# A two-layer graph network on one core: softmax operations for two groups at once, shorter tile-number loads, and a reordered turn start

## The reference

```
h = relu(layernorm(x))
# layer 0
xn = layernorm(h) * ln_w + ln_b
w_phys = (silu(rbf @ w1 + b1) @ w2 + b2) * cutoff[:, None]          # one record per edge
Q, K, V = xn @ wq + bq, xn @ wk + bk, xn @ wv + bv                  # 8 heads of 32
scores = sum(Q[row] * K[col], -1) / sqrt(32) * cutoff[:, None]      # per edge and head
attn = softmax(scores, axis=1)                                      # over the 8 heads of one edge
combined = xn[col] * w_phys + gate * (attn[..., None] * V[col])
x = x + h + segment_sum(combined, row) @ wo + bo
# layer 1
h = relu(layernorm(x)) @ W                                          # 4 heads of 64
e = leaky_relu(h_l[row] + h_r[col])                                 # softmax over the edges of a node
x = x + segment_sum(softmax_by_row(e)[:, :, None] * h[col], row)
```

## Time and profile before

| | us |
|---|---|
| median of 3 runs | 2323.9 |
| profiled execution | 2321.69 |
| its span | 2319.9 |
| PE busy, share of the span | 1961.0 (85%) |
| DVE busy | 1784.6 (77%) |
| ACT busy | 1479.1 (64%) |
| POOL busy | 1409.6 (61%) |

### The profile page before, as it was taken

One profiled execution on the slowest core, in us unless ns is written; L12 is line 12 of the kernel. 1 busy time (PEld: TensorE's weight loads), 2 busy tenths in 40 slices (PEclk: granted clock), 3 DMA queues, 4 the chain that ended last, 5 costly groups with the idle time before them and its releaser, 6 DMA issues.

```text
span 2319.9 us, 42068 instructions
## 1 busy us (share of the span) xinstructions
PE 1961.0 (85%) x9839; PEld 1426.4 (61%) x9840; DVE 1784.6 (77%) x4372; ACT 1479.1 (64%) x5220; POOL 1409.6 (61%) x1393
## 2 busy tenths in 40 slices
PE   5999999999958899998988889837777877877874
PEld 3777777777747677777777777624444444544542
DVE  5655444444359999998999999667999989999987
ACT  1585555555567777777777777446666666666660
POOL 0377777666776666665666664247666666666660
PEclk9999999999989999999999999977999989998997
DMA  8534444333389888888889882034433333343311
GB/s 279 160 133 144 157 146 146 138 138 131 113 291 301 299 290 292 298 293 280 296 290 308 291 296 76 19 93 113 110 107 107 105 108 100 105 110 104 106 32 56
DMA packets 162185, 403.69 MB, mean 174 GB/s; under 512 B 46887, under 2 KB 59099, under 8 KB 162108
## 3 DMA queue, kind: packets, MB, share of 16 engines
q0 software_dynamic: 79360, 276.09, 36.8%
q1 hardware_dynamic: 82748, 126.67, 17.4%
HBM read 343.89 MB, written 84.72 MB: 185 GB/s over the span
## 4 chain that ended last, share of the span: by engine, by line
PE 39%; DVE 28%; issue 16%; DMA 8%; ACT 4%; DVEq 4%; POOL 2%; SPq 0%; ACTq 0%; POOLq 0%
PE ps L1405 15%; DMA arena<-sorted_edges 6%; DVE gmx L1297 5%; PE ps L1391 4%; PE ps L1518 3%; PE ps L1521 3%; DVE arena L1329 3%; PE ps L1456 3%; PE ps L1533 2%; DVE work L1292 2%; DVE sc L1139 2%; DVE arena L1125 2%; DVEq L350 2%; PE ps L1643 2%; DVE arena L1132 2%
## 5 line engine op out<-in xcount | busy, mean ns | idle before, releaser
L630 POOL DMA_INDIRECT arena<-node_row,idxC x464 | 485.6, 1047 | 233.2 <-issue 136.8
L563 POOL DMA_INDIRECT sorted_edges<-work,pos_i x416 | 405.5, 975 | 236.5 <-issue 118.9
L1405 PE MATMUL ps<-w_sb,arena 128*128 128x256 f32 x1664 | 388.7, 386 | 0.2 <-ACT arena L674 0.2
L1643 PE MATMUL ps<-arena,hq 128*128 128x260 f32 x928 | 279.3, 428 | 96.2 <-DVE work L1292 92.8
L1069 DVE TENSOR_TENSOR work<-ps,b_bc 128x512 f32<-128x512 f32 x208 | 143.6, 691 | 273.6 <-PE ps L1405 273.6
L1405 PEld LDWEIGHTS ps<-w_sb,arena 128*128 128x128 f32 x1664 | 307.5, 190 | 72.2 <-issue 32.5
L585 POOL DMA_INDIRECT work<-node_kvx,idxB x232 | 245.7, 1059 | 154.4 <-DVE arena L1156 54.2
L585 POOL DMA_INDIRECT arena<-node_kvx,idxB x232 | 244.1, 1052 | 144.2 <-issue 51.2
L684 ACT ACTIVATE work<-work 128x256 f32<-128x256 f32 x416 | 187.5, 500 | 209.5 <-DVE work L1069 209.4
L1518 PE MATMUL ps<-arena,work 128*128 128x256 f32 x928 | 256.5, 400 | 59.1 <-issue 52.1
L1297 DVE TENSOR_REDUCE gmx<-ps 128x4 f32<-128x1024 f32 x232 | 282.5, 1218 | 28.4 <-PE ps L1618 28.4
(11 more groups left out here) (216 smaller groups left out, 3786.1 us busy)
## 6 DMA issues: line engine op xcount, KB each, us to landing
arena<-sorted_edges SPq DMA_DIRECT2D x232, 260.0 KB, 4.7
work<-sorted_rows SPq DMA_DIRECT2D x58, 256.0 KB, 3.6
arena<-in_edge_attr SPq DMA_DIRECT2D x25, 512.0 KB
node_kvx<-arena SPq DMA_DIRECT2D x24, 384.0 KB, 2.5
arena<-node_row,idxC POOLq DMA_INDIRECT x464, 3.3
sorted_edges<-work,pos_i POOLq DMA_INDIRECT x416, 2.5
sorted_edges<-arena SPq DMA_DIRECT2D x25, 260.0 KB
sorted_edges<-arena SPq DMA_DIRECT2D x1, 6240.0 KB
```

Source lines behind the costliest of these rows:

```text
L563: pool.indirect_dma_start(rec_dram[:, :], bass.IndirectOffsetOnAxis(ap=pos_i[:, 4 * q + c:4 * q + c + 1], axis=0), recA[:, q % 8, c, :], N ...
L630: pool.indirect_dma_start(row1_g[:, st.slot(16), j, :], None, row1_dram[:, :], bass.IndirectOffsetOnAxis(ap=idxC[:, batch(st).slot(4), st. ...
L1405: ins = pe.matmul(ps[:, 5 + t, half * H:(half + 1) * H], hidT[:, r, m, half, t * P:(t + 1) * P], w2_sb[:, m, :], start=m == 0, stop=m == 1)
L1643: ins = pe.matmul(agg1[r], oneh1[:, r16, j, :], msg1[:, r, j, :], start=j == 0, stop=j == GJ - 1)
```

## The change

In layer 0:

- The maximum over the heads, the exponentials, the reciprocal and the attention weights are taken for two groups at a time. DVE takes the maximum (one instruction over four columns) at the end of every even step, ACT the four exponentials in the odd step, DVE the reciprocal and the weights in the odd step. `msgA` is now made for the group five back (m), `msgP` still for the one four back; so PE's sums move from five back to six back, the addition to `acc0` from six to seven, and `msgP` has four slots, two of them in memory that held constants of the first stage (`mlp_only`). DVE runs one step longer at the end.
- DVE now adds to `acc0` ahead of the reciprocal, where before the reciprocal came first.
- DVE loads four tile numbers every fourth step instead of eight every eighth. PE loads one number every step, behind L1521's matmuls (`tile_of`), instead of eight at the first step ahead of L1518.
- `AHEAD` goes from 2 to 1: ACT copies a group's node numbers one step ahead of its one-hot matrix, not two. SP's load of records waits for `qk_cut` too.

In layer 1 DVE begins a turn's first step with the maxima; the load of tile numbers and the addition follow (`add_group` is the addition as it was).

The step ahead, and SP's load:

```
-AHEAD = 2
+AHEAD = 1
...
             def load_rec(st):
                 if not st.first(8):
                     sp.wait_ge(s("msgP_ready"), st.n - 7)
+                    sp.wait_ge(s("qk_cut"), st.n - 7)
```

The loads of tile numbers, and the new names that the code below calls:

```
-        def tiles_of(eng, k, lag, count=8):
+        def tiles_of(eng, k, lag, first):
...
-                gt_i[0:1, bass.ds(k * 8 + (16 - lag), count)], engines=(eng,), min_val=0, max_val=NT - 1,
+                gt_i[0:1, bass.ds(k * 8 + (16 - lag + first), 4)], engines=(eng,), min_val=0, max_val=NT - 1,
...
+        def tile_of(eng, k, lag, u):
+
+            _, values = nc.values_load_multi_w_load_instructions(
+                gt_i[0:1, bass.ds(k * 8 + (16 - lag + u), 1)], engines=(eng,), min_val=0, max_val=NT - 1,
...
+        def pair0(st):
+            return Step(st.k, st.u // 2, 4, NG // 2)
+
+        def msgP_of(st):
+            r = st.slot(4)
+            return msgP[:, r, :, :] if r < 2 else mlp_only[:, 2 * r - 4:2 * r - 2, :]
```

ACT in layer 0:

```
-                e = st.back(4)
-                if e.real():
+                if st.u % 2 and st.back(4).real():
+                    e = pair0(st.back(4))
                     act.wait_ge(s("sc_ready"), e.n + 1)
                     if not e.first(2):
                         act.wait_ge(s("attn"), e.n - 1)
...
+                    for r in (st.back(5).slot(4), st.back(4).slot(4)):
+                        for j in range(GJ):
+                            ins = act.activation(pe_[:, r, j, :], sc[:, r, j, :], ACT.Exp, bias=smax[:, r, j:j + 1],
+                                                 accum_out=psum_[:, r, j:j + 1])
                     ins.then_inc(s("exp0"), 1)
```

DVE in layer 0, from behind `msgP` on:

```
-                if st.u == 0:
-                    tiles[6] = tiles_of(DVE, st.k, 6)
+                if st.u % 4 == 0:
+                    tiles[7] = tiles_of(DVE, st.k, 7, st.u)
                 if a.real():
                     dve.wait_ge(s("qk"), na + 1)
                     dve.reduce_sum(sc[:, ra, :, :], heads(prod), axis=AX.X).then_inc(s("qk_sum"), 1)
-                if b.real():
-                    dve.wait_ge(s("exp0"), nb + 1)
-                    dve.reciprocal(prec[:, :], psum_[:, rb, :]).then_inc(s("prec"), 1)
                 if c.real():
...
                     dve.tensor_tensor(acc, acc, ps[:, 3 + c.slot(2), 0:H], ALU.add).then_inc(s("acc0_done"), 1)
...
+                if not both_in and b.real():
+                    e = pair0(b)
+                    re = m.slot(4)
+                    dve.wait_ge(s("exp0"), e.n + 1)
+                    dve.reciprocal(prec[:, :, :], psum_[:, re:re + 2, :]).then_inc(s("prec"), 1)
+                if not both_in and b.real():
+                    dve.wait_ge(s("prec"), e.n + 1)
...
+                if m.real():
+                    if not both_in:
+                        dve.wait_ge(s("attn"), pair0(m).n + 1)
+                    if not m.first(2):
+                        dve.wait_ge(s("agg0_ready"), m.n - 1)
...
+                if both_in and a.real():
+                    r0 = b.slot(4)
                     dve.wait_ge(s("qk_cut"), na + 1)
...
+                    dve.tensor_reduce(smax[:, r0:r0 + 2, :], sc[:, r0:r0 + 2, :, :], AX.X, ALU.max,
+                                      negate=True).then_inc(s("sc_ready"), 1)
```

PE in layer 0:

```
-                if st.u == 0:
-                    q_tiles[2] = tiles_of(PE, st.k, 2)
-                c = st.back(5)
+                c = st.back(6)
...
                     ins.then_inc(s("agg0_ready"), 1)
+                next_tile = tile_of(PE, st.k, 2, st.u)
                 b = st.back(2)
```

DVE in layer 1:

```
-                if st.u == 0:
-                    tiles[8] = tiles16(DVE, st.k, 11, 0)
                 c = st.back(11)
-                if c.real():
...
+                if c.real() and st.u:
+                    add_group(st, c)
                 if st.real():
                     bank = 1 + 2 * st.slot(2)
                     dve.wait_ge(s("hr_mm"), st.n + 1)
                     dve.reduce_max(gmx[:, b.slot(2), :, 1 + g],
                                    ps[:, bank:bank + 2, :].rearrange("p c (h e) -> p (c h) e", h=2),
                                    axis=AX.X).then_inc(s("gmax"), 1)
+                if st.u == 0:
+                    tiles[8] = tiles16(DVE, st.k, 11, 0)
+                if c.real() and st.u == 0:
+                    add_group(st, c)
```

More of the change, by code:

```diff
@@ L156, in gnn_kernel @@
         ones = sb("ones", [P, P])
-        w1_sb = sb("w1_sb", [P, H])
+        mlp_only = sb("mlp_only", [P, 4, H])
+        w1_sb, b2_bc, lnw_bc, lnb_bc = (mlp_only[:, i, :] for i in range(4))
         w2_sb = sb("w2_sb", [P, 2, H])
@@ L752, in layer0 @@
                     for j in range(GJ):
-                        v = sc[:, a.slot(2), j, :]
+                        v = sc[:, a.slot(4), j, :]
                         ins = act.activation(v, v, ACT.Copy, scale=recB[:, a.slot(8), j, H + 3:H + 4])
@@ L1139, in layer0 @@
                     dve.reduce_sum(sc[:, ra, :, :], heads(prod), axis=AX.X).then_inc(s("qk_sum"), 1)
-                if b.real():
-                    dve.wait_ge(s("exp0"), nb + 1)
-                    dve.reciprocal(prec[:, :], psum_[:, rb, :]).then_inc(s("prec"), 1)
                 if c.real():
-                    acc = tile(acc0, tiles[6][st.u])
-                    if not b.real():
+                    acc = tile(acc0, tiles[7][st.u % 4])
+                    if not c.first(1):
                         dve.wait_ge(s("acc0_done"), c.n)
@@ L1158, in layer0 @@
+                if m.real():
[3 more added lines that the diff above has]
+                        dve.wait_ge(s("agg0_ready"), m.n - 1)
+                    dve.tensor_tensor(heads(msgA[:, m.slot(2), :, :]), heads(kvx_g(m)[:, :, H:2 * H]),
+                                      attn[:, m.slot(2), :, :].unsqueeze(3).to_broadcast([P, GJ, NH0, HD0]),
                                       ALU.mult).then_inc(s("msgA_ready"), 1)
-                if a.real():
+                if both_in and a.real():
+                    r0 = b.slot(4)
@@ L1517, in layer0 @@
                     for j in range(GJ):
-                        pe.matmul(ps[:, 3 + r, 0:H], oneh[:, r8, j, :], msgP[:, r, j, :], start=j == 0, stop=False)
+                        pe.matmul(ps[:, 3 + r, 0:H], oneh[:, r8, j, :], msgP_of(c)[:, j, :], start=j == 0, stop=False)
                     pe.wait_ge(s("msgA_ready"), n + 1)
```

85 lines of the change are left out of this document (37 added, 48 removed).

## The result

The changed kernel took 2237.05 us (median; 2234.71 to 2238.14), beside 2323.83 us of the kernel before on the same chip: a ratio of 0.9624, 95% interval 0.9607 to 0.964, so 87 us faster. The forecast was 2249 us. The profiled execution took 2234.71 us, with a span of 2232.9 us.

A forecast was written before the change was run, and what follows sets the result against it. DVE was taken as the bound, with waits in layer 0. Terms -29 - 22.9 - 16 - 8 + 1.5 - 1 = -75.4 from 2321.7 give 2246.3, plus 2.2 for the median: 2249 us, range 2222 to 2287.

The forecast's parts named there:

- the stage's start and last step: Layer 0: one step more at the end costs half a step, +1.5 us.
- Pairs, -29: Layer 0, DVE: small operations for two groups at once save 0.25 us, 116 times, -29 us; bounds 0 and -48.
- DVE's load, -22.9: Layer 0: four tile numbers load in 0.94 us, under 1.03 us of cover, so the "issue" waits go, -22.9 us.
- PE's load, -16: Layer 0: PE's load of one fits under 0.84 us of weight loads; of DVE's 19.3 us waits, -16 us.
- (b): Layer 0: PE becomes the bound because part of each load shows, 0.4 us a step; 2271 us; chance 0.14.
- (d): Layer 0: PE's load has a fixed price near that of eight, 1.1 us showing each step; 2436 us; chance 0.04.
- Records, -8: Layer 0: with AHEAD 1 records arrive in time, taking a third of 26 us of small waits, -8 us; bounds 0, -20.
- the ring: Layer 0: record slot free 1.2 us into DVE's step, load landing 4.7 us later, ACT asking a good step after.
- rival (c): Layer 0: the loop of DVE and ACT, or a late transfer, sets the step at 3.25 us; 2283 us; chance 0.13.
- Layer 1, -1: Layer 1: maxima first bring DVE earlier only to wait for PE; 0.1 us, 14 times, -1 us; bounds -16, +1.
- rival (a): Layer 1: it gains its 1.1 us a turn too, if PE avoids slow matmuls; 2234 us; chance 0.10.

The follow-up runs named there:

- experiment 7: The kernel before with one change alone, the indices copied one step ahead instead of two: 2320.36 us, ratio to the kernel before 0.998.
- experiment 1: The changed kernel with layer 0's small operations done for one group each in every step again, not for two: 2259.45 us.
- 11: The changed kernel with DVE's reciprocal of a pair moved ahead of the addition of a finished sum: 2220.43 us.
- 2: The changed kernel with DVE's tile numbers loaded eight at a turn's start instead of four twice: 2259.37 us.
- 5: The kernel before with one change alone, PE loading one tile number a step: 2309.37 us, ratio to the kernel before 0.9929.
- 3: The changed kernel with PE's tile numbers loaded eight at a turn's start, ahead of the sums' matmuls, instead of one a step: 2318.95 us.
- 6: The changed kernel with the indices copied two steps ahead again: 2275.25 us.
- 8: The changed kernel with layer 1's turn beginning again with the load and the addition, as before: 2238.76 us.
- 9: The changed kernel with PE's aggregate at the fifth step of each layer-1 turn put off to the step after: 2224.54 us.
- 4: The changed kernel with both PE's and DVE's loads of eight tile numbers back at the turn's start: 2321.4 us.

## Why the prediction was right, and where it was off

Direction and mechanism came as forecast: DVE's waits in layer 0 went, DVE is the bound of each step. The time lies 12 us under the forecast, inside its range. By the traces, waits within layer 0's steps fell from 67.9 us (experiment 7) to 704.2 - 231 x 3.02 = 6.6, by 61 us, where -22.9 - 16 - 8 = -46.9 had been forecast: that is 14 us more. The pairs gave 25 us for 29 and layer 1 4.3 for 1, and the stage's start and last step cost 4 us for 1.5. Term by term:

- **Pairs, -29:** 22.4 measured (experiment 1), 25 by the steps. An even step was 2.82, as predicted; the odd one 3.22, not 3.19. The reciprocal's price was read as 0.19 us and is 0.21. That the addition no longer lies behind the reciprocal is a loss inside the change, as the text said; it is 0.12 us a pair, and 11 takes it back.
- **DVE's load, -22.9:** 22.3 (2). Four registers took 0.968 us for the 0.94 estimated, under the 1.03 of cover.
- **PE's load, -16:** 15.6 in the kernel before (5). One register took 0.302 us, for 0.27, and nothing of it shows: rivals (b) and (d) fell. The Trainium skill's floor of about 600 ns for a `tensor_load` ("DMA: Bandwidth & Descriptors", section "Latency and other measured facts") does not agree with the 297 ns shortest of 232 here. But the term is right only for the order in which it was taken: at the other end, with all else done, the same load costs 82 us (3).
- **Records, -8:** this is the term that was mis-sized. The text read `AHEAD` as a third of 26 us of small waits, with 20 as the most. Alone it took away 16 of the 26, of which 4.6 us were left as gain (7); taken away at the end it costs 38 (6). In the whole change nearly all of the small waits went. It had read the ring's parts (a slot free 1.2 us into a step, a load of 4.7 us, ACT a step later), but priced the waits of the trace of before, not the floor that the ring sets in the changed kernel: with two steps ahead, layer 0 could not have come under 3.22 us a step, and rival (c)'s 3.25 would have come about.
- **Layer 1, -1:** 1.7 (8); 4.3 by the maxima's first and last. The new wait for PE is there, 0.7 us a turn where about 1 was forecast, and 9 agrees with the reading behind it: with PE's order changed, 12.5 us come free, near the 15 us of rival (a).

Why the parts do not add: taken one at a time out of the changed kernel they cost 22.4 + 22.3 + 82 + 38 + 1.7 = 166 us, and the whole change gained 87. In the kernel before, DVE and PE stood still together at the start of each turn, and PE's stop showed only where its clock fell; the ring of the records, some 2.9 us by the estimate in 6, lay under DVE's 3.13 and showed in 16 us of small waits (7). In the changed kernel DVE's step is 3.02 us, and PE's stop (3) or the ring at 3.22 (6) stands above it at full length. So removing one leaves the next, and removing the last gives what the others had hidden. What stays open is why PE's load costs 0.8 us even in turns at full clock with both loads of eight back (4), while before it cost DVE nothing there: PE stands closer to DVE in the changed kernel, but by which of its waits was not tried.

## What to carry to other kernels

Price a change of several parts by the floors that would be left (the next engine, the next ring of waits with its length over the steps it spans), not by the waits that the trace of before happens to show: a wait that is small now can be the bound once its neighbours are gone. Two engines that stop at the same place of a loop hide each other's stop, so undoing one shows little, and a short stop of PE can cost as much again by its clock (1.65 us beside 1.7 in 3). After a pairing of small operations, look at what each result now waits for: one independent instruction moved between gave 16.6 us more.

## What the runs showed of the hardware

- Register loads: 0.302 us for one on PE, 0.968 us for four on DVE, 1.84 for eight: about 0.22 us for each further register. The sequencer takes them while the engine works on what is queued: of DVE's 0.968 us nothing showed as a wait, of its 1.84 us 0.82.
- TensorE after the same 1.9 us of idle time ran at the full granted clock in six of 27 turns and fell to half in 21 (experiment 3; by the durations of its matmuls, with the granted clock read in one turn of either kind); before, with the same stop, the matmuls were slow in 11 of 28 turns, and with `AHEAD` 1 in 19 (7). A small shift of the work around the stop changed how often. What decides it was not settled.
